# Four look-ups of a recommendation kernel: from TensorE to row-by-row transfers on SyncE's queue

## What is computed

```python
fidx = jnp.arange(F)[None, :]
sp_emb = emb_tables[fidx, sp_input]          # 2048 x 26 x 32
lin_vals = lin_tables[fidx, sp_input, 0]
lin_output = ds_input @ lin_w.T + lin_b + jnp.sum(lin_vals, axis=1, keepdims=True)
s = jnp.sum(sp_emb, axis=1)
bi_pooled = 0.5 * (s * s - jnp.sum(sp_emb * sp_emb, axis=1))
x = jnp.concatenate([bi_pooled, ds_input], axis=1)
h = jax.nn.relu(x @ w1.T + b1)
h = jax.nn.relu(h @ w2.T + b2)
out = jax.nn.sigmoid(h @ fw.T + fb + lin_output)
```

## Time and profile before

| | |
|---|---|
| median of three runs | 413.21 us (412.94 to 413.29) |
| the profiled execution, its own time | 413.37 us |
| its span in the trace | 411.6 us |
| TensorE busy (PE) | 405.3 us, 98% |
| VectorE busy (DVE) | 356.2 us, 87% |
| GpSimd busy (POOL) | 303.0 us, 74% |
| ScalarE busy (ACT) | 279.8 us, 68% |
| granted TensorE clock | 0.999 of full speed |

### The profile page before, as it was taken

The page is one execution under the profiler, slowest core; times in us unless marked ns, Lnnn a source line. Parts: engine busy times, 40 slices in busy tenths (PEclk is TensorE's granted clock), DMA queues, the critical chain, the costliest instruction groups (busy, mean ns, idle before and its releaser), DMA issues.

```text
span 411.6 us, 5945 instructions
## 1 busy us (share of the span) xinstructions
PE 405.3 (98%) x1910; PEld 347.3 (84%) x1910; DVE 356.2 (87%) x389; ACT 279.8 (68%) x500; POOL 303.0 (74%) x388
## 2 busy tenths in 40 slices
PE   7999999999999999998999999999999999999997
PEld 4888888888888888887888888888888887667764
DVE  7989999979699797879779999979779999989863
ACT  6999959555597655772975498767654786772243
POOL 5777778777777777876877787776777787676760
PEclk9999999999999999999999999999999999999999
DMA  8442251113311331215111512251115111101110
GB/s 216 113 152 28 27 179 28 26 24 98 117 28 20 92 122 18 27 15 186 28 22 21 188 27 31 41 179 24 18 26 180 24 15 13 12 12 12 13 13 0
DMA packets 17471, 24.85 MB, mean 60 GB/s; under 512 B 6061, under 2 KB 16399, under 8 KB 16402
## 3 DMA queue, kind: packets, MB, share of 16 engines
q1 hardware_dynamic: 8160, 19.55, 14.5%
q0 software_dynamic: 9280, 4.92, 10.9%
HBM read 24.40 MB, written 0.05 MB: 59 GB/s over the span
## 4 chain that ended last, share of the span: by engine, by line
PE 95%; ACT 2%; DVE 1%; issue 1%; DMA 1%; SPq 0%; DVEq 0%; ACTq 0%
PE cand L920 45%; PE cand L923 44%; PE bank_b L967 1%; DMA stage<-tabs 1%; PE cand L967 1%; PE bank_b L942 1%; PE bank_b L977 1%; PE bank_b L983 1%; PE cand L977 1%; ACT gates L746 0%; ACT high L713 0%; DVE masked L508 0%; PE bank_b L1106 0%; PE bank_a L942 0%; ACT h L799 0%
## 5 line engine op out<-in xcount | busy, mean ns | idle before, releaser
L388 POOL DMA_INDIRECT rows<-table,row_idx x285 | 273.2, 959 | 93.3 <-issue 64.2
L920 PE MATMUL cand<-high,gates 128*128 128x462 f32 x882 | 331.1, 375 | 2.3 <-DVE low L495 1.2
L923 PE MATMUL cand<-low,gates 128*128 128x462 f32 x882 | 328.8, 373 | 0.0
L920 PEld LDWEIGHTS cand<-high,gates 128*128 128x128 f32 x882 | 166.3, 189 | 28.8 <-issue 8.5
L923 PEld LDWEIGHTS cand<-low,gates 128*128 128x128 f32 x882 | 166.0, 188 | 19.9 <-issue 0.7
L516 DVE TENSOR_REDUCE picks<-masked 128x66 f32<-128x924 f32 x60 | 115.3, 1922 | 2.1
L508 DVE TENSOR_TENSOR masked<-cand,mask 128x924 f32<-128x924 f32 x62 | 69.3, 1118 | 32.3 <-PE cand L923 31.8
L746 ACT ACTIVATE gates<-distance,one 128x512 fp32r<-128x512 bf16 (+1 forms) x144 | 90.6, 680 | 0.0
L738 ACT ACTIVATE distance<-codes,minus_key 128x512 bf16<-128x512 f16 (+1 forms) x135 | 85.0, 680 | 0.1
L726 ACT COPY bank_b<-high 128x462 f32<-128x462 f32 x54 | 29.6, 549 | 50.6 <-DVE low L495 49.4
L483 DVE TENSOR_SCALAR gates<-bank_a,key_of 128x512 fp32r<-128x512 f32 (+1 forms) x94 | 60.9, 700 | 0.0
(11 more groups left out here) (118 smaller groups left out, 127.5 us busy)
## 6 DMA issues: line engine op xcount, KB each, us to landing
stage<-tabs SPq DMA_DIRECT2D x8, 1617.0 KB, 7.1
rows<-table,row_idx POOLq DMA_INDIRECT x285
codes<-codes_dram SPq DMA_DIRECT2D x27, 128.0 KB, 2.9
stage<-tabs SPq DMA_DIRECT2D x7, 231.0 KB, 4.6
codes<-codes_dram SPq DMA_DIRECT2D x5, 64.0 KB, 7.1
idx_raw<-sparse SPq DMA_DIRECT2D x1, 208.0 KB, 6.2
w_sb<-w2t SPq DMA_DIRECT2D x1, 128.0 KB
dense_sb<-dense_cols SPq DMA_DIRECT2D x1, 120.0 KB
```

Source lines behind the costliest of these rows:

```text
L388: pool.indirect_dma_start(out=to, out_offset=None, in_=table[:, :], in_offset=bass.IndirectOffsetOnAxis(ap=row_idx[:, at:at + 1], axis=0), ...
L920: first = nc.tensor.matmul(to, gate, high[f % 2][:, k, :], start=(k == 0), stop=False)
L923: last = nc.tensor.matmul(to, gate, low[f % 2][:, k, :], start=False, stop=(k == CHUNKS - 1))
```

## The change

`BY_ROW` takes four more look-ups from TensorE: field 6 of tiles 0 and 1 (out of job 24) and field 1 of tiles 12 and 13 (out of job 7). GpSimd does not get them. SyncE's queue fetches them, row by row: it loads 8 row offsets from the SBUF tile `col_rows` into registers (TENSOR_LOAD), and for each it computes an address (one fused register instruction, shown as ISA) and issues one transfer from the table in DRAM straight into one partition of `picks`. A transfer takes 37 numbers where 33 are wanted, so a place in `picks` is 37 wide (`ROW`). In all 64 register loads, 512 address instructions and 512 transfers are added to the queue, spread over it: behind the codes of each job from 4 on, 3 batches of 8 rows for a whole job and 2 for a half job (`ROWS_UNTIL`), until the 64th batch behind the codes of job 27. VectorE makes `col_rows` with one more instruction (so `col_raw` is no longer overwritten by the code computation), and the first `stage` load behind field 0 now also waits for it and for the clearing of `picks`. The sums of picks of blocks 0 and 3 wait for the rows. `LET` lets 126 and 100 hundredths of a gather go per half look-up instead of 122 and 96. The scratch for GpSimd's transfer descriptors is set to 4096 bytes of a partition instead of the default, 16384.

```diff
     CUT = [(2, 0), (3, 12), (5, 6), (4, 8)]
+    BY_ROW = [(6, 0), (1, 12)]
+    ROW = W + 4
+    OFF = CUT + BY_ROW
...
-    JOBS = [(f, b * TB + 2 * ((f, b * TB) in CUT)) for f in range(SUMMED) for b in range(BLOCKS)] + [(SUMMED, A0), (SUMMED, B0)]
+    JOBS = [(f, b * TB + 2 * ((f, b * TB) in OFF)) for f in range(SUMMED) for b in range(BLOCKS)] + [(SUMMED, A0), (SUMMED, B0)]
...
+    AT_ONCE = 8
+    ROW_LOADS = 2 * P // AT_ONCE * len(BY_ROW)
+    ROWS_UNTIL = [min(ROW_LOADS, sum(3 if n == TB else 2 for n in SIZE[4:j])) for j in range(NJ + 1)]
...
-    LET_OF = [[30, 30, 30, 440, 40, 40, 40, 340]] + [[122, 96] * n for n in SIZE[1:NJ - 4]] + [[140] * 8, [140] * 8, [140] * 8, [240] * 4]
+    LET_OF = [[30, 30, 30, 440, 40, 40, 40, 340]] + [[126, 100] * n for n in SIZE[1:NJ - 4]] + [[140] * 8, [140] * 8, [140] * 8, [240] * 4]
...
-        picks = sb("picks", [P, TILES, MMF, W])
+        picks = sb("picks", [P, TILES, MMF, ROW])
...
+            regs = [sp.alloc_register(f"row{i}") for i in range(AT_ONCE)]
+            flat = table.rearrange("r w -> (r w)")
+
+            def load_rows(n):
+
+                k, c = n // (2 * P // AT_ONCE), n % (2 * P // AT_ONCE) * AT_ONCE
+                f, t = BY_ROW[k]
+                line = (f * TILES + t) // 2
+                sp.load(regs, col_rows[line:line + 1, c:c + AT_ONCE])
+                for i in range(AT_ONCE):
+                    p = (c + i) % P
+                    at = sp.snap(regs[i], min_val=0, max_val=(CATS - 1) * W)
+                    sp.dma_start(picks[p:p + 1, t + c // P, f, :],
+                                 flat[f * ROWS * W:(f + 1) * ROWS * W][bass.ds(at, ROW)].unsqueeze(0)).then_inc(by_row_in[2 * k + c // P], 16)
+
             for j in range(2, 4):
                 load_codes(j)
+            sp.wait_ge(col_rows_made, 1)
+            sp.wait_ge(cut_cleared, len(CUT))
             for f in range(1, MMF):
...
                     load_codes(j)
+                    for n in range(ROWS_UNTIL[j], ROWS_UNTIL[j + 1]):
+                        load_rows(n)
...
             other_rows()
+            nc.vector.tensor_scalar(col_rows[:, :], col_raw[:, :], W, None, ALU.mult).then_inc(col_rows_made, 1)
...
+                for k in range(2 * len(BY_ROW)):
+                    if BY_ROW[k // 2][1] // TB == b:
+                        dve.wait_ge(by_row_in[k], 16 * P)
...
-    nc = bacc.Bacc("TRN2", target_bir_lowering=False, num_devices=1)
+    nc = bacc.Bacc("TRN2", target_bir_lowering=False, num_devices=1, dynamic_dma_scratch_size=4096)
```

More of the change, by code:

```diff
@@ L49, in build_deep_fm @@
     CUT = [(2, 0), (3, 12), (5, 6), (4, 8)]
+    BY_ROW = [(6, 0), (1, 12)]
+    ROW = W + 4
+    assert all(t % 2 == 0 and f < SUMMED for f, t in BY_ROW)
+    OFF = CUT + BY_ROW
     FIELDS = [[f for f, c in CUT if t in (c, c + 1)] + list(range(PEF[t], F)) for t in range(TILES)]
@@ L80, in build_deep_fm @@
     assert all(h * MUL >> SHIFT == h // J for h in range(J * CHUNKS))
-    JOBS = [(f, b * TB + 2 * ((f, b * TB) in CUT)) for f in range(SUMMED) for b in range(BLOCKS)] + [(SUMMED, A0), (SUMMED, B0)]
+    JOBS = [(f, b * TB + 2 * ((f, b * TB) in OFF)) for f in range(SUMMED) for b in range(BLOCKS)] + [(SUMMED, A0), (SUMMED, B0)]
     NJ = len(JOBS)
-    SIZE = [TB - 2 * ((f, t // TB * TB) in CUT or (f, t // TB * TB + 2) in CUT or t == B0) for f, t in JOBS]
+    SIZE = [TB - 2 * ((f, t // TB * TB) in OFF or (f, t // TB * TB + 2) in OFF or t == B0) for f, t in JOBS]
     WHOLE = [sum(n == TB for n in SIZE[:j + 1]) for j in range(NJ)]
+    AT_ONCE = 8
+    ROW_LOADS = 2 * P // AT_ONCE * len(BY_ROW)
+    ROWS_UNTIL = [min(ROW_LOADS, sum(3 if n == TB else 2 for n in SIZE[4:j])) for j in range(NJ + 1)]
+    assert ROWS_UNTIL[NJ - 6] == ROW_LOADS
     PAIR = [sum(SIZE[:j]) // 2 for j in range(NJ)]
@@ L187, in build_deep_fm @@
         col_hi = sb("col_hi", [R // 2, 2 * P], i32)
+        col_rows = sb("col_rows", [R // 2, 2 * P], i32)
         col_code = sb("col_code", [R // 2, 2 * P], fp16)
@@ L279, in build_deep_fm @@
         cut_cleared = sem("cut_cleared")
+        col_rows_made = sem("col_rows_made")
+        by_row_in = [sem(f"by_row_in{k}") for k in range(2 * len(BY_ROW))]
         rested = sem("rested")
@@ L379, in _ @@
                             pool.wait_ge(codes_out, 16)
+                            pool.wait_ge(col_rows_made, 1)
                         else:
@@ L444, in find_codes @@
                     dve.wait_ge(col_step, 6)
-                    nc.vector.tensor_scalar(col_raw[:, :], col_hi[:, :], SHIFT, None, ALU.arith_shift_right).then_inc(col_step, 1)
+                    nc.vector.tensor_scalar(col_hi[:, :], col_hi[:, :], SHIFT, None, ALU.arith_shift_right).then_inc(col_step, 1)
                     dve.wait_ge(col_step, 7)
-                    nc.vector.scalar_tensor_tensor(col_code[:, :], col_raw[:, :], P, col_wrap[:, :], ALU.mult,
+                    nc.vector.scalar_tensor_tensor(col_code[:, :], col_hi[:, :], P, col_wrap[:, :], ALU.mult,
                                                    ALU.add).then_inc(col_step, 1)
@@ L512, in pick @@
                 dve.wait_ge(picked, p + 1)
-                to = picks[:, t:t + 2, f, :]
+                to = picks[:, t:t + 2, f, 0:W]
                 if f == SUMMED:
@@ L549, in sum_picks @@
                 dve.wait_ge(cut_cleared, len(CUT))
-                nc.vector.tensor_reduce(pick_sums[:, c, BOTH], picks[:, c, 0:parts, :].rearrange("p t f w -> p t w f"),
+                for k in range(2 * len(BY_ROW)):
+                    if BY_ROW[k // 2][1] // TB == b:
+                        dve.wait_ge(by_row_in[k], 16 * P)
+                nc.vector.tensor_reduce(pick_sums[:, c, BOTH], picks[:, c, 0:parts, 0:W].rearrange("p t f w -> p t w f"),
                                         AX.X, ALU.add).then_inc(picks_reduced, 1)
@@ L576, in sum_tile @@
                 dve.wait_ge(gathered[t % RING], gathered_until(t))
-                sum_rows(t, t, 0, GF[t], picks[:, t, SUMMED, :], pick_sq[:, t, SUMMED, :])
+                sum_rows(t, t, 0, GF[t], picks[:, t, SUMMED, 0:W], pick_sq[:, t, SUMMED, :])
             def make_x(m):
@@ L630, in _ @@
             other_rows()
+            nc.vector.tensor_scalar(col_rows[:, :], col_raw[:, :], W, None, ALU.mult).then_inc(col_rows_made, 1)
             for f, t in CUT:
-                nc.vector.memset(picks[:, t:t + 2, f, :], 0.0).then_inc(cut_cleared, 1)
+                nc.vector.memset(picks[:, t:t + 2, f, 0:W], 0.0).then_inc(cut_cleared, 1)
             nc.vector.tensor_copy(sub_id[:, :], sub_i[:, :]).then_inc(consts_made, 1)
@@ L759, in square_picks @@
                 act.wait_ge(cut_cleared, len(CUT))
+                for k in range(2 * len(BY_ROW)):
+                    if BY_ROW[k // 2][1] // TB == b:
+                        act.wait_ge(by_row_in[k], 16 * P)
                 nc.scalar.activation(pick_sq[:, c, 0:SUMMED, :], picks[:, c, 0:SUMMED, 0:E],
```

## The result

The changed kernel takes **441.4 us** (439.4 to 442.6, four runs) against 413.1 us for the kernel before on the same chip: ratio 1.068 (95% interval 1.064 to 1.072), slower. The forecast, 403.0, had the wrong sign, and the time is 1.4 us above the range. The profiled execution is the fastest of the four, 439.43 us with a span of 437.7.

A forecast was written before the change was run, and what follows sets the result against it. TensorE, busy 98% of the span, was taken as the bound: 413.4 − 11.8 (look-ups) + 1.4 (wait at job 7) + 0.3 (GpSimd allowance) = 403.3 us profiled, 403.0 forecast; own range 402.0 to 405.5, widened up to 440.

The forecast's parts named there:

- the price of a batch: SyncE's queue: one register load, 8 address steps and 8 issues take 3.6 us, between 2.4 and 7.4.
- The issue: SyncE's queue: issuing one row's transfer takes 0.29 us, at most 0.47.
- The address step: SyncE's queue: computing one row's address takes 0.07 us, between 0 and 0.25.
- The load: SyncE's queue: loading 8 registers takes 0.7 us, between 0.04 and 1.6.
- the limit: SyncE's queue: up to 3.8 us a batch, late tables of fields 2, 4 and 7 stay hidden from TensorE.
- the break-even: SyncE's queue: at 3.95 us a batch the gain is used up.
- The rule as printed: TensorE at the queue's pace: beyond 3.8 us a batch, every further 0.1 us costs 6.4 us.
- The second rival: SyncE's queue becomes the bound: load 1.6 us, batch 4.5 us, 448 us, or 4.2 us and 429; chance 39%.
- The third rival: Rows wait behind table data: SyncE stalls up to 5 us per table, 0.5 us a batch; within the second rival's 39%.
- the new wait for `low`: Job 7, now a half job: TensorE waits for field 2's low part and loses 1.4 us.
- the last gather: GpSimd: the last gather starts at 389 to 390 us and its rows land at 392, wanted at 394.0.
- the smaller scratch and the start: GpSimd's smaller descriptor scratch costs nothing; the first `stage` load waits about 1 us more, also costing nothing.

The follow-up runs named there:

- Experiment 1: Changed kernel with constant transfer addresses, so no register load, address instruction or MOVE; all 512 transfers stay but fetch wrong rows: 402.65 us against 412.99 for the kernel before.
- experiments 3 and 4: Changed kernel with four registers to a load, twice as many loads: 465.97 us; with sixteen to a load, counts halved and rounded up: 431.5 us.
- experiment 5: Changed kernel with its 64 batches of 8 spread over jobs 4 to 31 instead of 4 to 27: 408.88 us against 413.07 for the kernel before.

## Why the prediction was wrong

- **The step that failed** is the price of a batch on SyncE's queue: 8 × (0.29 + 0.07) + 0.7 = 3.6 us. It is 4.2 by itself and 4.3 on average. *The issue* was right: 0.23 and 0.05 behind it, 0.28 against 0.29. *The address step* carried the miss: 0.14 against 0.07, because it is two instructions, each with its gap, and not one. That is 8 × 0.07 = 0.56 us of the 0.6. *The load* is 0.80 + 0.03 against 0.7, which is 0.13 more, and the issues give 0.08 back. With the load alone put right the batch would be 3.7 us, below the limit; with the address step alone put right it is 4.1, above the break-even. Experiment 1, without both, has the gain back; experiments 3 and 4, which change the loads, moved the time with them. No run takes out the address step alone: its share is read from the trace.
- **The limit** of 3.8 us and the break-even of 3.95 were sound in kind: two batches a job cost nothing, 4.3 us a batch lost all. By the rule as printed, 4.3 us give 413.2 + 64 × 0.35 = 435.6 us; the profiled execution has 439.4. Of the 3.8 us, 1.4 are rounding: the limit is 3.77 before it is rounded to 3.8, and unrounded the same rule gives 403.1 + (16.88 + 11 + 64 × 4.3 − 261.6 − 7.6) = 437.0. The other 2.4 us: the table of field 7 left at 304.5 and not at the 303.1 of this sum. In experiment 1 it leaves at 260.7, so in the changed kernel it is 43.8 us late and not 41.5, and of that the kernel lost 439.4 − 402.6 = 36.8, so 7.0 were covered and not 7.6; the kernel without the loss is 402.6 and not 403.1. By which share the lower clock adds to this no run isolates, and the 2 us by which the median of the runs is longer than the profiled execution I can't place. So the range's end, "up to 440 us (a batch of 4.37)", was missed though the batch was below 4.37.
- **The second rival** ("the queue becomes the bound", 39%) is what happened: its mechanism, its place and its signs, ScalarE's idle time ahead of `high` and TensorE waiting for `low`. Of its numbers the load of 1.6 us was wrong and the address step was too. The third rival, rows waiting behind a table's data, did not happen: the longest of 512 issues is 319 ns, and behind six of the tables the rows are issued while the table is in flight.
- **Right**: the 11.8 us of the look-ups, the new wait for `low` (at most 1.3 us against 1.4), the last gather, and that the smaller scratch and the start cost nothing. Experiment 1 has them together at 402.65, where 403.0 was forecast. Two small slips changed nothing: the fourth matmul of a half job starts three steps of 0.21 us, so 0.6 and not 0.8, behind its first, which would have made the wait for `low` 1.2 to 1.3 us; and 122 look-ups of 7 chunks are 854 pairs of matmuls, as the trace has, and not 826.
- **What I did not compute** is the pace by job. I compared sums up to a table's due time, with a margin of 5%. At my own price three batches and the codes are 3 × 3.6 + 0.4 = 11.2 us against 11.8, hardly any room, and the two of a half job are 7.6 against 5.9, too much. At the measured 4.3 they are 13.3 and 9.0. Two or two and a half batches to a whole job would have done; experiment 5 made 32.5 us of that.
- **The price of a load.** Measured are 0.56, 0.79 and 1.19 us for 4, 8 and 16 registers, which is some 0.35 us and 0.053 for each register. The Trainium skill, in "Runtime: NRT & Kernel Launch", section Instruction fetch mechanics, has about 200 ns for each register, in a passage on registers loaded from HBM; by that, as an estimate, 16 would be 3.2 us. This load is from SBUF, and for it the measurement decides against the figure. The Trainium skill, in "DMA: Bandwidth & Descriptors", section Latency and other measured facts, has a floor of some 600 ns, and the load of four registers, 562 ns, is near it.

## What to carry to other kernels

Work moved to a queue that is nearly idle still has to fit between what that queue must deliver: compare the queue's time for one step of the main loop with that step, not only the sums, and put the added work where the next urgent transfer isn't behind it. Of an instruction that the trace has never shown, count how many instructions it becomes, with the gap behind each. If a forecast hangs on such a price within 10% of the break-even, say that it is open, and price the even spread too: here the same 512 transfers gave 441 or 403 us by their place and their grouping alone.

## What the runs showed of the hardware

- A transfer with an address from a register is three instructions on SyncE, 0.42 us a row (fused step 44 ns, MOVE 29 ns, issue 228 ns, the rest gaps); with a constant address it is 0.30 us.
- A register load from SBUF is 562, 793 and 1192 ns for 4, 8 and 16 registers, so bigger is better: 0.14, 0.10 and 0.07 us a register.
- 512 transfers of 148 bytes beside table loads and 290 gathers cost TensorE nothing that shows (402.65 us against a forecast of 403.0 that charged nothing for them; with the wanted rows, spread, 403.42).
- Where TensorE waited, its granted clock was lower too: 0.87 in the stretch with 127 matmuls of 192, 1.00 where all 192 ran. After a wait of 6.2 us it was 0.50 (1.2 GHz) for the next 13 matmuls, 0.385 us apart instead of 0.21.
